# TensorE's fillers in the delta solve, halved and dealt out between the two value heads' applies

## What is computed

```
state = state * d_t
Sk    = einsum('bhi,bhij->bhj', k_t, state)
delta = (v_t - Sk) * b_t
state = state + einsum('bhi,bhj->bhij', k_t, delta)
o     = einsum('bhi,bhij->bhj', q_t, state)
```

## Time and profile before

| | |
|---|---|
| median of 3 runs | 1928.41 us |
| the profiled execution, its own time | 1928.7 us |
| its span, first to last instruction | 1926.8 us |
| TensorE, matmuls busy | 91% of the span |
| VectorE busy | 75% |
| ScalarE busy | 58% |
| GpSimd busy | 38% |
| mean granted TensorE clock | 0.968 of full speed |
| layer 1's heads 1 to 15 | one each 77.8 to 78.7 us |

### The profile page before, as it was taken

How to read it: one execution, slowest core, us unless ns; L and a number is a source line. 1 busy time by engine, 2 the same in 40 slices (tenths; PEclk the granted TensorE clock), 3 DMA queues, 4 the chain that set the end, 5 groups by cost and what they waited for, 6 DMA issues and landing times.

```text
span 1926.8 us, 34411 instructions
## 1 busy us (share of the span) xinstructions
PE 1745.5 (91%) x13208; PEld 1346.4 (70%) x13208; DVE 1451.5 (75%) x2389; ACT 1124.0 (58%) x2154; POOL 731.5 (38%) x474
## 2 busy tenths in 40 slices
PE   7899999999989878989999899998898999989986
PEld 5676676767656656867778677776776777867775
DVE  7888888888764687777877777777777787777853
ACT  3353535353444556676766767667667676686752
POOL 3213122222230543371643725526347164371540
PEclk9999999999989969999999999999999999999988
DMA  3010101111032001111011010110101101101000
GB/s 134 33 63 31 63 32 62 42 52 54 10 98 71 18 1 34 37 42 34 23 34 56 24 34 23 34 56 24 34 28 51 34 24 34 55 24 34 7 2 22
DMA packets 51449, 75.44 MB, mean 39 GB/s; under 512 B 3392, under 2 KB 41792, under 8 KB 51184
## 3 DMA queue, kind: packets, MB, share of 16 engines
q1 hardware_dynamic: 51312, 73.55, 11.8%
HBM read 72.29 MB, written 1.25 MB: 38 GB/s over the span
## 4 chain that ended last, share of the span: by engine, by line
PE 39%; ACT 15%; DVE 11%; issue 5%; POOL 2%; ACTq 0%; POOLq 0%; DVEq 0%
PE bank L729 7%; PE bank L903 6%; PE bank L858 5%; DVE d_sil L1318 5%; PE bank L746 3%; DVE d_Rb L1388 3%; PE bank L796 2%; PE bank L806 2%; ACT d_TT L1148 2%; POOL d_dec L1637 2%; ACT d_V L1106 2%; PE bank L879 1%; PE bank L881 1%; PE bank L880 1%; PE bank L810 1%
## 5 line engine op out<-in xcount | busy, mean ns | idle before, releaser
L1637 POOL TENSOR_TENSOR d_dec<-d_dec,d_qk 128x384 f32<-128x384 f32 x128 | 162.6, 1295 | 564.1 <-DVE d_N L1353 564.1
L1318 DVE SCALAR_TENSOR_TENSOR d_sil<-d_pre,d_w,d_sil 128x1024 f32<-128x1024 f32 x192 | 301.4, 1570 | 5.0 <-ACT d_pre L1078 4.7
L729 PE MATMUL bank<-xnT,d_w 128*128 128x512 f32 x480 | 246.3, 649 | 1.8
L1372 DVE CAST_PREDICATED d_X<-tables_sb,bank 128x512 bf16<-128x512 int32 x192 | 134.4, 701 | 137.8 <-PE bank L796 125.9
L189 PE MATMUL bank<-xnT,a_w 128*128 128x512 f32 x512 | 237.7, 598 | 0.0
L1144 ACT ACTIVATE d_T<-bank 128x512 bf16<-128x512 f32 x160 | 98.3, 615 | 113.8 <-PE bank L806 111.7
L489 POOL TENSOR_TENSOR a_hidc<-a_hid,a_comb 128x512 f32<-128x512 f32 x32 | 44.4, 1387 | 293.7 <-DVE a_hid L336 293.7
L729 PEld LDWEIGHTS bank<-xnT,d_w 128*128 128x128 f32 x480 | 92.3, 209 | 83.6 <-issue 83.6
L189 PEld LDWEIGHTS bank<-xnT,a_w 128*128 128x128 f32 x512 | 91.2, 193 | 79.2 <-issue 79.2
L1629 POOL TENSOR_TENSOR x_sb<-x_sb,d_yrs 128x1024 f32<-128x1024 f32 x32 | 73.7, 2325 | 160.6 <-DVE d_yrs L1431 160.6
L858 PEld LDWEIGHTS bank<-d_W,d_N 128*128 128x128 f32 x1024 | 123.4, 194 | 14.5 <-issue 6.7
(11 more groups left out here) (210 smaller groups left out, 4457.9 us busy)
## 6 DMA issues: line engine op xcount, KB each, us to landing
d_dec<-decay_scratch SPq DMA_DIRECT2D x32, 512.0 KB, 5.4
a_w<-w SPq DMA_DIRECT2D x16, 897.0 KB, 4.6
d_w<-w SPq DMA_DIRECT2D x16, 776.0 KB, 4.7
a_comb<-comb_scratch SPq DMA_DIRECT2D x16, 512.0 KB, 5.4
d_dec<-decay_scratch SPq DMA_DIRECT2D x32, 256.0 KB, 6.0
d_wo<-w SPq DMA_DIRECT2D x16, 256.0 KB, 3.0
f_w<-w SPq DMA_DIRECT2D x8, 256.0 KB, 4.2
tables_sb<-tables SPq DMA_DIRECT2D x1, 1056.0 KB, 8.7
```

What stands on the lines that cost most here:

```text
L729: last = pe.matmul(psum[bank][:, :], cols(slot, (c * KT + k) * P, P), xnT[:, k, h * HALF:(h + 1) * HALF], start=(k == 0), stop=(k == KT - 1))
L1318: dve.scalar_tensor_tensor(sil[c][:, :, :], pre[c % 2][:, :, tap:tap + S], cols(slot, OC + 4 * c + tap, 1), sil[c][:, :, :], ALU.mult, ALU ...
L1372: dve.copy_predicated(left(Xp[lv][:, v], lv), mask.unsqueeze(1).broadcast_to([P, 8, 64]).rearrange("p n (g w) -> p n g w", w=lv), psum[4 + ...
L1637: pool.tensor_tensor(g, g, qk[b % 2][:, :, :], ALU.mult).then_inc(s["p_done"], 1)
```

## The change

Each of the fillers `p(3, 1)`, z(0) and z(1) can now be issued in two halves: `project` and `project_z` take `parts`. Part 0 does the waits, part 1 signals that the result is ready. The fillers get four places in a step instead of two: `ahead` of apply v=0, `between` the two applies, `behind` apply v=1 (the old first place), and `closing`, after the residuals (the old second place). z(0) moves from step 4 to steps 0 and 1, z(1) from step 5 to steps 3 and 4. No instruction is added or taken away on any engine.

```diff
-            def project(slot, i, c, h):
+            def project(slot, i, c, h, parts=(0, 1)):
...
-                for k in range(KT):
+                for k in parts:
...
-                last.then_inc(s["proj_ready"], 1)
-
-            def project_z(slot, i, n):
-                if n < 2:
+                if 1 in parts:
+                    last.then_inc(s["proj_ready"], 1)
+
+            def project_z(slot, i, n, parts=(0, 1)):
+                if 0 not in parts:
+                    pass
+                elif n < 2:
                     pe.wait_ge(s["pre_done"], i * 8 + 5 + n)
                     need(pe, s["acc_done"], (i - 2) * 4 + 3 + n)
...
-                for q in range(2):
+                for q in parts:
...
-                    z = lambda n: (lambda: project_z(nxt[1], nxt[2], n))
-                    more = [([p(3, 1)], []), ([q(0, 0)], [q(0, 1)]), ([q(1, 0)], [q(1, 1)]), ([], []),
-                            ([z(0)], []), ([z(1)], [])]
+                    p31 = lambda k: (lambda: project(nxt[1], nxt[2], 3, 1, (k,)))
+                    z = lambda n, half: (lambda: project_z(nxt[1], nxt[2], n, (half,)))
+                    ahead[0], between[0], behind[0] = [p31(0)], [p31(1)], [z(0, 0)]
+                    between[1], behind[1] = [z(0, 1)], [q(0, 0)]
+                    between[2], behind[2], closing[2] = [q(0, 1)], [q(1, 0)], [q(1, 1)]
+                    between[3] = [z(1, 0)]
+                    between[4] = [z(1, 1)]
                 invert(i, fill)
                 for c in range(2):
                     for a in range(3):
-                        for v in range(2):
-                            apply(i, v, c, a)
-                        for f in more[3 * c + a][0]:
+                        k = 3 * c + a
+                        for f in ahead[k]:
+                            f()
+                        apply(i, 0, c, a)
+                        for f in between[k]:
+                            f()
+                        apply(i, 1, c, a)
+                        for f in behind[k]:
                             f()
...
-                        for f in more[3 * c + a][1]:
+                        for f in closing[k]:
                             f()
```

More of the change, by code:

```diff
@@ L716, in _ @@
         def _(pe):
-            def project(slot, i, c, h):
+            def project(slot, i, c, h, parts=(0, 1)):
                 bank = (2 * c + h) % 4
-                if c < 2:
+                if 0 not in parts:
+                    pass
+                elif c < 2:
                     need(pe, s["sz_done"], (i - 1) * 4 + bank + 1)
@@ L747, in project_z @@
                                          cols(slot, OZ + k * 2 * P, 2 * P), start=(k == 0), stop=(k == KT - 1))
-                last.then_inc(s["z_ready"], 1)
+                if 1 in parts:
+                    last.then_inc(s["z_ready"], 1)
             def norms(i, c, h):
@@ L924, in body @@
                         fill[li][half].append(lambda n=n: project_out(*before, n, nxt))
-                more = [([], []) for _ in range(6)]
+                ahead, between, behind, closing = ([[] for _ in range(6)] for _ in range(4))
                 if nxt:
```

## The result

The changed kernel takes 1875.41 us (median of 4, 1874.74 to 1876.01), beside 1928.24 us for the kernel before: a ratio of 0.973, interval 0.9717 to 0.9742. The prediction was 1879 with a range of 1867 to 1902.

What follows compares the result with a forecast made beforehand. TensorE's matmuls fill 1745.5 of 1926.8 us, with VectorE setting the pace in the solve's middle. 1928.7 less 45 (14 x 3.1 + 1.7) for filled waits and 5 for clock falls gives 1879 us, range 1867 to 1902.

Steps and rivals of the forecast that it cites:

- The waits: Delta solve of heads 1 to 14: fillers put into TensorE's waits bring the outputs 3.1 us earlier a head.
- Step 0: Start of the solve: p(3,1)'s halves fill the waits around the applies; the first residual goes out 0.9 us earlier.
- Steps 1 and 2: VectorE runs without a break, 0.9 us early; step 2's first apply waits about 0.4, the first norm hardly for `square`.
- Step 3: Half of z(1), 0.89 us, between the applies for waits of 0.28 and 0.20; residual only 0.6 us early.
- Steps 4 and 5: End of the solve: 1.78 us fillers behind the applies go; VectorE is late, step 5's first apply waits 0.95 us.
- the outputs' lost cover: Without z(1) hiding the copy of W, the outputs wait for ScalarE, 0.44 + 0.64 us after step 5's apply.
- Head 0: Convolution steps stretch and VectorE alone sets the middle; only steps 3 to 5 gain, some 1.7 us.
- The clock: Falls from 2.4 to 1.2 GHz around the inversion's start cost 0.8 us each; 0 to 10 us possible, 5 taken.
- Rival 1: VectorE sets steps 4 and 5 fully and takes gain back: 14 x 1.9 + 1.7 = 28, 1900 us; chance 0.12.
- Rival 2: A second clock fall per head at the solve's end, where waits stand close together: 34 us gained, 1895 us; chance 0.07.
- Rival 3: The halves wait for their inputs where they now stand, so nothing is gained: 1928 us; chance 0.02.
- Rival 4: GpSimd's running mask holds a VectorE convolution step in the solve, 3.9 us a head: 1940 us; chance 0.04.

Runs made afterwards that it cites:

- experiment 4: Changed kernel with z(1) whole behind step 5's applies again, as in the kernel before; 1899.81 us, ratio 0.985 to the kernel before.
- experiments 5 to 8: Changed kernel with step 4's SiLU behind left_over, 1876.84 us; changed kernel with 128 or 256 columns more, 1886.27, 1892.65; kernel before with 256 more, 1931.71.
- experiment 12: Changed kernel with three VectorE convolution steps in the solve's middle cut to two columns in heads 1 to 15; 1872.31 us, ratio 0.971 to the kernel before.
- experiment 1: Kernel before with only p(3,1) in halves, ahead of and between step 0's applies; 1910.67 us, ratio 0.991.
- experiment 3: Changed kernel with the fillers moved but not halved; 1896.26 us, ratio 0.984 to the kernel before.

## Why the prediction was right

The mechanism was the forecast one: fillers in front of the waits shorten each head, and the falls of the clock change in number with it. The total came as near as it did in part by luck, since misses of both signs cancelled.

**The waits.** Forecast 14 x 3.1 = 43, measured 39.3 (2.81 a head). Inside the solve the replay was close: first apply to outputs 21.9 forecast, 22.06 measured. The rest is behind it. From the outputs to the next first apply it was 77.81 - 25.28 = 52.53 us and is 75.00 - 22.06 = 52.94 (a distance of 75.00 us, where 74.7 was forecast); I had counted 0.25 for `ahead` and got 0.41. One part shows in the rows: the first pair of output matmuls, which now follows a wait, took 0.32 us to the next start (1326.74 to 1327.06) where pairs before took 0.22.

**Step by step.** Step 0: first residual 2.3 us behind the first apply as worked out. Steps 1 and 2: the wait of 0.4 ahead of step 2's first apply came as 0.35, that for `square` didn't show. Step 3: right in its result for a reason half understood; experiment 4 showed that without the half of z(1) ScalarE's copy of W would have let the residual go only 0.12 us earlier. Steps 4 and 5: 0.95 us of waiting forecast ahead of step 5's first apply, 0.83 measured by the starts (2.67 us from the residual at 1322.98 to the apply at 1325.65, less the 1.84 that a residual takes); the outputs' lost cover as forecast, 0.44 + 0.64 us (1325.65 to 1326.74 is 1.09).

**Head 0.** Forecast 1.7, measured 3.3. Half of the 3.3 us is the 1.7 us from layer 0, which is chance. The half of `p(3, 1)` ahead of the first apply takes 1.0 us back, and from first apply to outputs 2.7 us are gained (39.3 to 36.6). Of these, 0.7 us are there by step 3's first apply (27.35 us behind the first apply, 26.66 after), for which I had counted nothing, and 2.0 come in steps 3 to 5, where I had 1.7. The clock differs there too (1.2 GHz from 701.3 to 721.8 us before; after, from 699.6 to 713.3 and from 716.6 to 720.0), so how much of the 2.7 us the filled waits made stays open.

**The clock.** I gave it 5 us, the middle between 0 and 10, and it was 10: the two misses, 4 us less from the waits and 5 more from the falls, cancelled, and that was luck. The place (the thin stretch at the inversion's start) and the price (0.8) were right. What I could not say was how many falls stay, and experiments 5 to 8 show why no row of the kernel before tells it: kernels whose stretch is the same have from one to thirteen. The 1.7 us more in head 0 make up the rest of the difference between 1879 and 1875.

**The rivals.** Rival 1 (VectorE takes it back) is bounded by experiment 12 to 0.47 us a head. Rival 2 (a second fall at the solve's end) didn't come: no distance has two. Rival 3 is out by the rows. Rival 4's hold was 0.13 to 0.16 us in 13 of heads 1 to 14, none in the other. The sign given for it, a convolution step over 2 us in a middle head, holds for the solve only: in the inversion, beside GpSimd's work, both kernels have steps of 2.3 us (at 1319.52 before, at 1281.29 after), which the prediction had not looked at.

Not tried: whether the distances that draw falls follow a rule that could be worked out ahead, and whether moving the first head in time, at the same distance, changes their number.

## What to carry to other kernels

Where an engine alternates between two independent chains, its fillers belong in front of the instruction that waits, cut to the length of the wait; a filler behind it lengthens the chain for everyone who needs the next result. Follow the second engine's copies before counting a filler as free or as a cost, for a copy may hide it. And before judging a change by its total, count the falls of the clock in both traces and compare distances that have none: here a real gain of 0.7 us a head measured as nothing, and 0.85 us of added work a head as a third of its length.

## What the runs showed of the hardware

The same stretch of TensorE's work, some 1.5 of 3.4 us busy, was followed by a fall to 1.2 GHz in 13 of 14 heads or in one of 14, and what differed was the distance between heads (with it the time at which each head stands, which was not separated): 13 falls at 77.8 and at 74.3 us, one or two at 75.0 and 78.7, four to nine in the seven other kernels, at 74.5 to 77.1. A fall made a distance 0.5 to 0.9 us longer (0.46 in one of experiment 1, 0.92 in one of experiment 3). With the stretch filled by one projection (3.28 of 3.40 us busy) there was none, at three distances. And a VectorE instruction with two inputs in SBUF that was issued while a GpSimd instruction ran ended some 1.08 us behind that instruction's end, in head 0 before and beside the masks after. In the changed kernel's trace that holds for 147 of the 148 convolution steps and SiLUs that began beside running GpSimd work.
